# A three-branch attention and expert tower on one core: two casts change engine, and the work between batches is put in another order

## The chip, the cores and the metric

The kernel runs on one core of a Trainium2 chip. The metric is the device time of one execution in microseconds (us). A difference of about 0.3% is what a measurement of this kernel can tell from no change.

## What is computed

Eight sequences of 512 tokens are embedded (token, instruction and argument tables, then a layer norm) into 64 channels. Attention with 16 heads follows. Each head has one query (96 wide, 64 of them rotated by position) and three branches of keys and values: all earlier tokens, 128 tokens chosen by a score, and a window of 128 tokens. The three results are summed with one gate per batch and branch, projected, and added to the input. A layer norm and a mixture of eight experts (two per token) close the tower. Cut to the attention:

```python
        qr = _rope((cq @ Wq_rope).reshape(B, T, N_HEAD, ROPE).transpose(0, 2, 1, 3), cos, sin)
        q = jnp.concatenate([qn, qr], -1)
...
        o1 = _attn(q, k1, v1, causal[None, None])
...
        o2 = _attn(q, ks, vs)
...
        o3 = _attn(q, kw, vw, winmask[None, None])
```

## The kernel before, in words

**Precision.** Operands of the score, value and projection products are split into a high half in fp16 and a low half (the rest, in fp16), and three products stand for one.

**Loops.** Eight batches run one after the other, with 16 heads each. A head has four tiles of 128 queries. Each engine has its own program with the same loops (`heads`, then the last two heads, then `behind`, which holds the work between two batches). Every engine works through its own queue in order, and semaphores tie the queues together. One pass over a head is `turn` on TensorE (L1388), ScalarE (L647) and VectorE (L1090). At step t of four in the turn of head h, tile (t+3) mod 4 gets its scores, tile t+1 is transposed, and tile t gets its value product. So steps 1 to 3 already score tiles 0 to 2 of head h+1.

**A tile's way.** TensorE writes scores into one of two PSUM tiles S (L1336). VectorE masks them and takes the maxima (`maxima`, L996). ScalarE takes the exponentials (`probs`, L624). TensorE transposes them into PT (L1361, L1368). ScalarE takes the high half out (`take_hi`, L636) and VectorE the low half (`take_lo`, L1006). TensorE multiplies with the values (L1383). At a head's end VectorE normalises and gates the three branches (`combine`: a reciprocal L1013, the small product `coef` L1015 whose two inputs lie in SBUF, and L1018), and GpSimd adds the branches up (`branch_sum`, L472 and L474).

**Queries and keys of head h+2** are made during the turn of head h. TensorE projects the keys (`k_proj`, L1287) and the queries (`q_proj`, L1278) into the one tile X, and ScalarE copies each out (`evac_k`, `evac_q`, L565). GpSimd rotates them (L423, L424, L427, L428), casts them to fp16 (L456 the keys, L445 the queries) and subtracts that from the original for the low half (L459, L448). The sync engine then transposes `kparts` and `qparts` by DMA into `kh` and `qh` (L318, L327). TensorE needs both at step 1 of the next turn. GpSimd's order in one turn is: keys, queries, `low_values` (L479, the low half of the next head's values, whose high half is ScalarE's `high_values`), `branch_sum`. In the last batch `normalise` (L487 to L498) stands once in two turns between the queries and `low_values`. TensorE waits for its result when it transposes rows (L1348).

**Between two batches.** The last two heads of a batch also project the next batch's first two heads (`lead`). Nine value products (`value`, L1416) fill `vall`: 0 to 3 for all tokens, 4 to 7 for the window, 8 for the chosen ones. Four stand in the last head and five in `behind`. There TensorE also transposes the attention result (`attended`, L1442), scores the next head's tiles 0 and 1, projects the output (`project`, L1473), scores tile 2 and transposes tile 0. VectorE's `residual` (L1131) reads the projection, and TensorE waits for it at the end of `behind` (L1515).

Of the kernel before, what the change touches and what calls it, by code (L numbers as in the profile page):

```python
# [6 lines left out]
P = 128  # L7
# [25 lines left out]
def tower(nc, d, out):  # L33
# [5 lines left out]
    with ctx:  # L39
# [185 lines left out]
        VBANK = [S[0][:, 0:512], S[0][:, 512:1024], S[1][:, 0:512], S[1][:, 512:1024]]  # L225
        ZT = PT[:, 7 * P:8 * P]
# [140 lines left out]
        def _(g):  # L367
# [71 lines left out]
            def split_query(par, b, hh):  # L439
# [5 lines left out]
                g.tensor_copy(qparts[:, 0], qs[par][:]).then_inc(s["q_high"], 1)  # L445
                g.wait_ge(s["q_high"], H + 1)
# [3 lines left out]
            def split_key(par, b, hh):  # L450
# [5 lines left out]
                g.tensor_copy(kparts[:, 0, :, NOPE:P], kk[par][:, :, NOPE:P]).then_inc(s["k_high"], 1)  # L456
                g.wait_ge(s["k_high"], H + 1)
# [3 lines left out]
            def query(par, b, hh, x):  # L461
                rope_q(par, b, hh, x)
                split_query(par, b, hh)

            def key(par, b, hh, x):
                rope_k(par, b, hh, x)
                split_key(par, b, hh)
# [55 lines left out]

            def heads(b, rows=False):
                with g.Fori(0, NH // 2 - 1) as hp:
                    for par in range(2):
                        key(par, b, hp * 2 + (par + 2), xbase(b) + hp * 4 + x_index(par, "kp"))
                        query(par, b, hp * 2 + (par + 2), xbase(b) + hp * 4 + x_index(par, "qp"))
                        if rows and par == 0:
                            normalise(hp, xn_b[:])  # L530
                        low_values(1 - par, b, hp * 2 + (par + 1))
                        branch_sum(par, b, hp * 2 + par)
# [30 lines left out]
        def _(act):  # L563
# [48 lines left out]

            def high_values(par, b, hh):
# [33 lines left out]
            def turn(b, h, xb, p, last, nxt=None, rows=None):  # L647
# [3 lines left out]
                for t in range(NT):  # L651
                    u = p * NT + t
                    if t == 0 and last < 1:
                        evac_k(p, xb + x_index(0, "kp"), H + 1)
                        evac_q(p, xb + x_index(0, "qp"), H + 1)
                    if t == 2 and last < 2:
                        high_values(1 - p, b, h + 1)
                    if nxt is not None:
# [3 lines left out]
                    if nxt is not None and last == 2 and t >= 2:  # L662
                        if t == 2:
                            act.wait_ge(s["v_split"], b * NH + NH)
                        value(b + 1, (t - 2) * 2)
# [10 lines left out]
            def value(b, i):  # L676
                act.wait_ge(s["v_psum"], b * 9 + i + 1)
                if i < 4:
                    nc.scalar.activation(vall[:, i, :], VBANK[i % 4], ACT.Copy, scale=qkinv[:, 2:3]).then_inc(s["v_act"], 1)
                else:  # L680
                    copy(vall[:, i, :], VBANK[i % 4]).then_inc(s["v_act"], 1)
# [16 lines left out]
            def behind(b, nxt, U, first):  # L698
# [5 lines left out]
                value(b, 4)  # L704
# [16 lines left out]
            value(0, 0)  # L721
            value(0, 2)
# [60 lines left out]
        def _(dve):  # L783
# [239 lines left out]
            def value(b, i):  # L1023
                dve.wait_ge(s["v_psum"], b * 9 + i + 1)
                if i < 4:
                    v.tensor_scalar(vall[:, i, :], VBANK[i % 4], qkinv[:, 2:3], None, ALU.mult).then_inc(s["v_dve"], 1)
                else:
                    v.tensor_copy(vall[:, i, :], VBANK[i % 4]).then_inc(s["v_dve"], 1)
# [61 lines left out]
            def turn(b, H, p, last, nxt=None, rows=None):  # L1090

                U = H * NT
                for t in range(NT):
# [19 lines left out]
                    if nxt is not None and last == 2 and t >= 2:  # L1113
                        if t == 2:
                            dve.wait_ge(s["v_split"], H + 1)
                        value(b + 1, (t - 2) * 2 + 1)
# [16 lines left out]
            def behind(b, U, first):  # L1133
                value(b, 5)
# [6 lines left out]
                maxima(1, 1, U + 1)  # L1141
                if not first:
                    residual(b - 1)
                maxima(2, 2, U + 2)
                take_lo(0, 0, U)
# [5 lines left out]
            value(0, 1)  # L1151
            value(0, 3)
# [57 lines left out]
        def _(pe):  # L1210
# [177 lines left out]
            def turn(h, H, xb, p, last, b=None, nxt=None, rows=None):  # L1388
# [3 lines left out]
                for t in range(NT):  # L1392
                    u = p * NT + t
                    if last < 1 and t == 0:
                        k_proj(h + 2, xb + x_index(0, "kp"))
                    i = t if last == 1 else t + 4
# [7 lines left out]
                    if last < 1 and t == 0:  # L1404
                        q_proj(h + 2, xb + x_index(0, "qp"))
# [4 lines left out]
                    if nxt is not None and last == 2 and t >= 2:  # L1410

                        value(b, (t - 2) * 2)
                        value(b, (t - 2) * 2 + 1)
                    values(u, t, p, U + t, H)

            def value(b, i):  # L1416

                if i >= 4 and i % 2 == 0:
                    pe.wait_ge(s["v_act"], b * 5 + (i - 4) // 2 + 1)
                if i >= 4 and i % 2 == 1:  # L1420
                    pe.wait_ge(s["v_dve"], b * 4 + (i - 5) // 2 + 1)
                if i == 0:
                    pe.wait_ge(s["k1_moved"], b * 2 + 2)
                if i < 4:
                    for c, a in ((0, 0), (0, 1), (1, 0)):
                        last = mm(VBANK[i % 4], k1T[:, c, i * P:(i + 1) * P], wvh[:, a], start=(c + a == 0), stop=(c == 1))
                elif i < 8:
                    for a in range(2):
                        last = mm(VBANK[i % 4], xh[:, (i - 4) * P:(i - 3) * P], wvwh[:, a], start=(a == 0), stop=(a == 1))
                else:  # L1430
                    for a in range(2):
                        last = mm(VBANK[i % 4], selh[:], wvsh[:, a], start=(a == 0), stop=(a == 1))
                last.then_inc(s["v_psum"], 1)

            def behind(b, nxt, H, first):
# [9 lines left out]
                for i in range(4, 9):  # L1445
# [233 lines left out]
```

## Time and profile before

| what | value |
|---|---|
| time, median of 3 runs | 1868.04 us (1863.59 to 1869.03) |
| the profiled execution: its own time, its span | 1866.17 us, 1864.2 us |
| busy share: TensorE, VectorE, ScalarE, GpSimd | 76%, 79%, 65%, 77% |
| granted TensorE clock over the span, in the heads | 0.964, 1.00 |
| VectorE waits for TensorE's scores (L996) | 118.0 us in 142 waits |
| TensorE waits for the transposed queries (L1336) | 108.7 us in 98 waits |
| GpSimd waits for VectorE's combine (L472) | 53.6 us in 17 waits |
| transposed queries and keys, issue to landing | 3.0 us and 3.4 us |

The profile is of one execution. Its span runs from the first to the last instruction and is 2.0 us shorter than that execution's time, and its time is 1.9 us under the median. Four engines are busy about equally, so busy shares alone don't show what sets the pace. That has to be read from a turn's timeline and from who waits for whom.

### The profile page before, as it was taken

The page shows a single profiled execution, that of the slowest core. Times are in us where ns is not written, and L with a number is a line of the kernel's source. Part 1 is how long each engine was busy: PE and PEld are TensorE (multiplying, and loading weights), DVE is VectorE, ACT ScalarE, POOL GpSimd, SP SyncE. Part 2 cuts the span into 40 slices and gives each one's busy share as a digit, 9 for nine tenths or more (in the row PEclk, how much of TensorE's full clock was granted, in tenths as well). Part 3 has the DMA queues.
Part 4 walks back from the last instruction along what each step waited for, and adds up shares of the span by engine and source line. Part 5 has one row for each costly group of instructions (what it writes and reads, how often), then busy time and mean ns, then how long its engine had stood idle before and what let it go on. Part 6 is the DMA issues. An engine that isn't in the chain of part 4 may idle for free.

```text
span 1864.2 us, 64283 instructions
## 1 busy us (share of the span) xinstructions
PE 1417.9 (76%) x19368; PEld 1139.9 (61%) x19368; DVE 1474.7 (79%) x4982; ACT 1219.8 (65%) x3280; POOL 1436.9 (77%) x2126
## 2 busy tenths in 40 slices
PE   1041588888888888888888888888888888888878
PEld 0021476667776766676766677666767666767643
DVE  5738588878888788878887888788878887878745
ACT  0041377767776777767776777677767776777634
POOL 6775588868887788778877888688868887899610
PEclk9985799999999999999999999999999999999989
DMA  5110222222222222222222222222222221233200
GB/s 92 23 26 16 47 53 53 54 55 51 51 51 44 61 56 52 44 58 53 54 46 57 54 51 51 54 51 53 56 50 54 51 56 38 50 68 68 53 4 21
DMA packets 327553, 92.03 MB, mean 49 GB/s; under 512 B 321104, under 2 KB 323024, under 8 KB 327520
## 3 DMA queue, kind: packets, MB, share of 16 engines
q1 hardware_dynamic: 324448, 88.48, 24.1%
q0 software_dynamic: 3072, 3.15, 1.0%
q8 instruction: 15, 0.25, 0.1%
q14 instruction: 18, 0.15, 0.0%
HBM read 6.51 MB, written 1.05 MB: 4 GB/s over the span
## 4 chain that ended last, share of the span: by engine, by line
POOL 38%; DVE 21%; issue 18%; PE 10%; DMA 7%; POOLq 2%; ACT 1%; DVEq 1%; SPq 0%; ACTq 0%
DMA qh<-qparts 7%; DVE S L996 6%; POOL big L424 6%; POOL big L393 5%; DVE big L1006 5%; POOL big L423 4%; POOL kparts L459 4%; POOL qparts L448 3%; POOL kparts L456 2%; DVE negm L996 2%; POOL qparts L445 2%; POOL kk L427 2%; PE S L1336 2%; DVE coef L1015 2%; POOL kk L428 2%
## 5 line engine op out<-in xcount | busy, mean ns | idle before, releaser
L624 ACT ACTIVATE big<-S,negm 128x128 f32<-128x128 f32 (+3 forms) x1536 | 578.4, 454 | 116.9 <-DVE negm L996 116.9
L1006 DVE SCALAR_TENSOR_TENSOR big<-PT,big 128x384 f16<-128x384 f32 (+3 forms) x1024 | 477.5, 502 | 55.8 <-ACT big L636 41.1
L636 ACT ACTIVATE big<-PT 128x384 f16<-128x384 f32 (+3 forms) x1024 | 422.3, 453 | 141.1 <-PE PT L1361 107.0
L1336 PE MATMUL S<-k1T,qh 128*128 128x128 f16 (+3 forms) x1536 | 297.3, 302 | 122.6 <-DMA qh<-qparts 108.7
L996 DVE CUSTOM_DVE_ANT_0 S<-S,mask_c,unscale 128x128 f32<-128x128 f32 (+3 forms) x512 | 285.3, 557 | 129.5 <-PE S L1336 118.0
L1336 PE MATMUL S<-kh,qh 128*128 128x128 f16 (+1 forms) x3072 | 320.3, 241 | 0.0
L1383 PEld LDWEIGHTS O<-vh,big 128*128 128x128 f16 x8064 | 276.5, 96 | 22.8 <-DVE big L1018 8.6
L1383 PE MATMUL O<-vh,big 128*128 128x33 f16 x8064 | 282.8, 178 | 7.3 <-DVE big L1018 5.5
L1368 PE MATMUL PT<-cst,big 128*128 128x128 f32 x1408 | 246.9, 280 | 20.6 <-DVE big L1006 18.3
L1336 PEld LDWEIGHTS S<-kh,qh 128*128 128x128 f16 x3072 | 227.7, 99 | 56.5 <-issue 2.3
L1361 PE MATMUL PT<-cst,big 128*128 128x128 f32 x1280 | 230.3, 279 | 13.9 <-DVE big L1006 12.6
L996 DVE CUSTOM_DVE_ANT_0 S<-S,cst,kfix 128x256 f32<-128x256 f32 (+1 forms) x512 | 233.0, 455 | 0.0
L996 DVE DVE_READ_ACCUMULATOR2_ANT negm<- 128x1 f32 x1536 | 217.5, 142 | 0.2
L1336 PEld LDWEIGHTS S<-k1T,qh 128*128 128x128 f16 x1536 | 110.1, 98 | 162.3 <-issue 118.2
L1368 PEld LDWEIGHTS PT<-cst,big 128*128 128x128 f32 x1408 | 160.4, 142 | 51.2 <-issue 45.2
L996 DVE CUSTOM_DVE_ANT_0 S<-S,mask_c,kfix 128x128 f32<-128x128 f32 x512 | 181.6, 355 | 0.0
L1283 PE MATMUL X<-wqh,cqT 128*128 (+1 forms) x1536 | 116.6, 222 | 74.4 <-ACT kk L565 58.0
L565 ACT ACTIVATE qs<-X 128x512 f32<-128x512 f32 x128 | 76.6, 598 | 146.6 <-PE X L1283 146.6
L1361 PEld LDWEIGHTS PT<-cst,big 128*128 128x128 f32 x1280 | 146.8, 143 | 25.8 <-DVE big L1006 15.0
L448 POOL TENSOR_TENSOR qparts<-qs,qparts 128x512 f16<-128x512 f32 x128 | 148.1, 1157 | 18.6
L1283 PEld LDWEIGHTS X<-wqh,cqT 128*128 128x128 f16 x1536 | 91.8, 98 | 109.2 <-issue 105.7
L459 POOL TENSOR_TENSOR kparts<-kk,kparts 128x480 f16<-128x480 f32 x128 | 141.0, 1102 | 18.6
(295 smaller groups left out, 2449.2 us busy)
## 6 DMA issues: line engine op xcount, KB each, us to landing
lat_b<-lat_all SPq DMA_DIRECT2D x8, 448.0 KB, 3.1
qh<-qparts SPq DMA_TRANSPOSE x128, 3.0
kh<-kparts SPq DMA_TRANSPOSE x128, 3.4
xnT_all<-xnT_b SPq DMA_DIRECT2D x14, 128.0 KB, 2.5
xn_b<-xn_all SPq DMA_DIRECT2D x8, 128.0 KB, 2.8
xnT_b<-xnT_all SPq DMA_DIRECT2D x8, 128.0 KB, 2.3
out_dram<-h_all SPq DMA_DIRECT2D x8, 128.0 KB, 2.0
xn_all<-xn_b SPq DMA_DIRECT2D x7, 128.0 KB, 2.0
```

The lines of the kernel that those rows point to most:

```text
L424: g.tensor_tensor(tmp[:, 1, 0:tiles, :], v, sin5[:, 0:tiles, :], ALU.mult).then_inc(part, 1)
L448: g.tensor_tensor(qparts[:, 1], qs[par][:], qparts[:, 0], ALU.subtract).then_inc(s["q_split"], 1)
L459: g.tensor_tensor(kparts[:, 1, :, NOPE:P], kk[par][:, :, NOPE:P], kparts[:, 0, :, NOPE:P], ALU.subtract).then_inc(s["k_split"], 1)
L624: last = nc.scalar.activation(pr[par][:, lo:lo + n], S[par][:, lo:lo + n], ACT.Exp, bias=negm[par][:, k:k + 1], scale=-1.0)
L636: last = nc.scalar.activation(pT[par][:, 0, lo:lo + n], PT[:, lo:lo + n], ACT.Copy, scale=PSCALE)
L996: last = v.tensor_tensor_reduce(out=z, in0=z, in1=m, scale=unscale[:] if k == 0 else kfix[:], scalar=3.0e38, op0=ALU.add, op1=ALU.min, acc ...
L1006: v.scalar_tensor_tensor(pT[par][:, 1, lo:lo + n], PT[:, lo:lo + n], PSCALE, pT[par][:, 0, lo:lo + n], ALU.mult, ALU.subtract).then_inc(s[ ...
L1283: last = mm(X[:, t * QW:(t + 1) * QW], cqT[:, c, t * P:(t + 1) * P], wqh[:, a].rearrange("c h q -> c (h q)")[:, ds(h * QW, QW)], start=(c ...
L1336: last = mm(z[:, lo:lo + n], qh[par][:, c, t * P:(t + 1) * P], keys[:, a, :], start=(c + a == 0), stop=(c == 1))
L1361: last = tp(PT[:, lo:lo + P], src[:, lo:lo + P], ident)
L1368: last = tp(PT[:, lo:lo + P], src[:, lo:lo + P], ident)
L1383: last = mm(o, w[:, c, blocks[i] * P:(blocks[i] + 1) * P], vh[p][:, a, v0 + i, :], start=(j == 0), stop=(j == len(parts) - 1))
```

## The change

GpSimd no longer casts queries and keys in the turns of heads 0 to 13. ScalarE does it, at steps 2 and 3 of the turn. GpSimd's order in a turn is written anew (`prepare`), with the two additions of `branch_sum`, now of the head before, set between the steps of the rotation. `low_values` and, in the last batch, `normalise` stand at its end. On TensorE `q_proj` goes from step 0, behind the scores, to the start of step 1, and on ScalarE `evac_q` and `high_values` stand at the start of step 1. The value products come in another order (`VORDER`), six of them in the last head from step 1 on and three in `behind`. The output projection goes behind the scores of tile 2 and the transposes of tile 0, and `residual` with it. The work at the batch border on GpSimd stays as it was, casts included.

```diff
+        VORDER = [4, 5, 6, 7, 8, 0, 1, 2, 3]
...
+            def prepare(b, h, hh, par, rows=None, add=True):
+                x, H = xbase(b) + h * 2, b * NH + hh
...
+                g.wait_ge(s["x_evac"], x + x_index(0, "kp") + 2)
+                g.tensor_tensor(kt[:, 0], k[:, :, NOPE:HD], cos5, ALU.mult)
+                g.tensor_tensor(kt[:, 1], k[:, :, NOPE:HD], sin5, ALU.mult).then_inc(s["rope_tk"], 1)
+                if add:
+                    g.wait_ge(s["comb_done"], b * NH + h + 1)
...
+                    g.tensor_tensor(osum[:], o[:, :, 0, :], o[:, :, 1, :], ALU.add).then_inc(s["osum_part"], 1)
+                g.wait_ge(s["rope_tk"], H + 1)
...
+                g.wait_ge(s["x_evac"], x + x_index(0, "qp") + 2)
+                g.tensor_tensor(qt[:, 0, 0:NT], q[:, :, NOPE:HD], cos5[:, 0:NT], ALU.mult)
+                g.tensor_tensor(qt[:, 1, 0:NT], q[:, :, NOPE:HD], sin5[:, 0:NT], ALU.mult).then_inc(s["rope_tq"], 1)
+                if add:
...
+                    g.tensor_tensor(o_b[:, :, ds((h - 1) * VD, VD)], osum[:], o[:, :, 2, :], ALU.add).then_inc(s["osum_done"], 1)
+                g.wait_ge(s["rope_tq"], H + 1)
...
+                low_key(par, b, hh)
+                low_query(par, b, hh)
+                low_values(1 - par, b, hh - 1)
+                if rows is not None:
+                    normalise(rows, xn_b[:])
...
+            def high_key(par, H):
+                act.wait_ge(s["rope_k"], H + 1)
+                act.wait_ge(s["k_turned"], H * 16 + 16)
+                copy(kparts[:, 0, :, NOPE:P], kk[par][:, :, NOPE:P]).then_inc(s["k_high"], 1)
+            def high_query(par, H):
+                act.wait_ge(s["rope_q"], H + 1)
+                act.wait_ge(s["q_turned"], H * 16 + 16)
+                copy(qparts[:, 0], qs[par][:]).then_inc(s["q_high"], 1)
...
                     if t == 0 and last < 1:
                         evac_k(p, xb + x_index(0, "kp"), H + 1)
+                    if t == 1 and last < 1:
                         evac_q(p, xb + x_index(0, "qp"), H + 1)
-                    if t == 2 and last < 2:
+                    if t == 1 and last < 2:
                         high_values(1 - p, b, h + 1)
+                    if t == 2 and last < 1:
+                        high_key(p, H + 2)
+                    if t == 3 and last < 1:
+                        high_query(p, H + 2)
...
-                    if nxt is not None and last == 2 and t >= 2:
+                    if nxt is not None and last == 2 and t >= 1:
...
                     if last < 1 and t == 0:
                         k_proj(h + 2, xb + x_index(0, "kp"))
+                    if last < 1 and t == 1:
+                        q_proj(h + 2, xb + x_index(0, "qp"))
...
-                    if last < 1 and t == 0:
-                        q_proj(h + 2, xb + x_index(0, "qp"))
...
                 scores(1, 1, 0, H * NT + 1)
+                scores(2, 2, 0, H * NT + 2)
+                if not first:
+                    pe.wait_ge(s["oT_act"], b * 2)
+                    pe.wait_ge(s["oT_dve"], b * 2)
+                turn_probs(0, 0, H * NT)
                 if not first:
                     project(b - 1, H)
-                scores(2, 2, 0, H * NT + 2)
-                turn_probs(0, 0, H * NT)
```

## Rows read from the trace of the kernel before

**Rows 1.** Busy time by engine in one head's turn (window, us, busy us).

```profile
508.85:519.99 11.14, 9.11 (x145) 7.77 (x143) 9.97 (x38) 8.75 (x24) 9.92 (x16) 1.00 0.27 52
```

**Rows 2.** One of GpSimd's groups: busy us, mean ns | idle before, releaser.

```profile
L456 POOL CAST kparts<-kk 128x480 f16<-128x480 f32 x128 | 74.7, 584 | 33.7 <-POOL kk L428 33.4 <-DMA kh<-kparts 0.3
```

**Rows 3.** GpSimd's timeline: start us, length us, engine, line, operation.

```profile
513.68 0.73 POOL L423 TENSOR_TENSOR big<-qs,cst 128x256 f32<-128x256 f32 x1
...
516.25 0.61 POOL L445 CAST qparts<-qs 128x512 f16<-128x512 f32 x1 [0.19 <-POOL qs L428]
517.00 1.16 POOL L448 TENSOR_TENSOR qparts<-qs,qparts 128x512 f16<-128x512 f32 x1
518.12 0.71 POOL L479 TENSOR_TENSOR vh<-vall,vh 128x288 f16<-128x288 f16 x1
```

**Rows 4.** VectorE's timeline over two heads; idle before, releaser in brackets.

```profile
512.04 1.02 DVE L1006 SCALAR_TENSOR_TENSOR big<-PT,big 128x384 f16<-128x384 f32 x2
...
517.43 0.76 DVE L1015 TENSOR_TENSOR coef<-rinv,gate_all 128x12 f32<-128x12 f32 x1
...
518.79 0.75 DVE L996 CUSTOM_DVE_ANT_0 S<-S,mask_c,unscale 128x512 f32<-128x512 f32 x1
...
522.38 0.36 DVE L996 CUSTOM_DVE_ANT_0 S<-S,mask_c,unscale 128x128 f32<-128x128 f32 x1 [0.89 <-PE S L1336]
...
523.20 1.01 DVE L1006 SCALAR_TENSOR_TENSOR big<-PT,big 128x384 f16<-128x384 f32 x2
...
528.47 0.84 DVE L1015 TENSOR_TENSOR coef<-rinv,gate_all 128x12 f32<-128x12 f32 x1
...
530.20 0.76 DVE L996 CUSTOM_DVE_ANT_0 S<-S,mask_c,unscale 128x512 f32<-128x512 f32 x1 [0.20 <-issue]
```

**Rows 5.** ScalarE's timeline in the first of these heads.

```profile
511.51 0.87 ACT L636 ACTIVATE big<-PT 128x384 f16<-128x384 f32 x2 [0.49 <-PE PT L1361]
...
513.08 0.45 ACT L565 ACTIVATE vh<-vall 128x288 f16 x1
513.47 0.98 ACT L636 ACTIVATE big<-PT 128x512 f16<-128x512 f32 x2
...
515.41 0.29 ACT L636 ACTIVATE big<-PT 128x128 f16<-128x128 f32 x1
```

**Rows 6.** VectorE's timeline in the head before a batch ends.

```profile
575.68 0.75 DVE L996 CUSTOM_DVE_ANT_0 S<-S,mask_c,unscale 128x512 f32<-128x512 f32 x1
...
579.50 1.02 DVE L1006 SCALAR_TENSOR_TENSOR big<-PT,big 128x384 f16<-128x384 f32 x2 [0.47 <-ACT big L636]
```

**Rows 7.** ScalarE's timeline in the same head.

```profile
577.29 1.31 ACT L624 ACTIVATE big<-S,negm 128x512 f32<-128x512 f32 x3 [2.38 <-DVE negm L996]
578.48 0.61 ACT L565 ACTIVATE qs<-X 128x512 f32<-128x512 f32 x1
578.96 0.89 ACT L636 ACTIVATE big<-PT 128x384 f16<-128x384 f32 x2
```

**Rows 8.** The tile coef: ns min/median/max, first and last start.

```profile
L1015 DVE TENSOR_TENSOR coef<-rinv,gate_all x128: 170/754/867, 235.0 to 1783.8; 128x12 f32<-128x12 f32 x128
```

**Rows 9.** TensorE's timeline between two batches.

```profile
600.56 1.09 PE L1442 MATMUL PT<-cst,o_b 128*128 128x128 f32 x8 [0.65 <-POOL o_b L474]
...
604.80 3.79 PE L1473 MATMUL O<-wproj,oT 128*128 128x64 f32 x32 [0.89 <-ACT oT L565]
...
610.20 0.60 PE L1292 MATMUL X<-wkw,xh 128*128 x8 [0.30 <-issue]
```

**Rows 10.** VectorE's timeline, last batch: row statistics, two heads apart.

```profile
1640.42 0.59 DVE L1034 BATCH_NORM_STATS2 bst<-h_all 128x6 f32 x4
...
1665.00 0.60 DVE L1034 BATCH_NORM_STATS2 bst<-h_all 128x6 f32 x4
```

**Rows 11.** GpSimd's timeline, last batch: first and last step of a normalisation.

```profile
1645.44 0.23 POOL L493 TENSOR_SCALAR lnr<-lnmv 128x4 f32<-128x4 f32 x1
...
1647.45 0.61 POOL L498 TENSOR_TENSOR xn_b<-xn_b,lnr 128x256 f32<-128x256 f32 x1
```

More of the change, by code:

```diff
@@ L437, in rope_k, with high_query @@
                 rope(kk[par], rt[1], s["rope_tk"], s["rope_k"], 5, b * NH + hh + 1)
-            def split_query(par, b, hh):
+            def high_query(par, b, hh):
                 H = b * NH + hh
@@ L534, in _ @@
+            def heads(b, rows=False):
+                prepare(b, 0, 2, 0, 0 if rows else None, add=False)
+                with g.Fori(0, NH // 2 - 2) as hp:
+                    prepare(b, hp * 2 + 1, hp * 2 + 3, 1)
+                    prepare(b, hp * 2 + 2, hp * 2 + 4, 0, hp + 1 if rows else None)
+                prepare(b, NH - 3, NH - 1, 1)
+                branch_sum(1, b, NH - 3)
             with g.Fori(0, B - 1) as b:
@@ L720, in _ @@
                 lead(i, 0)
-            value(0, 0)
-            value(0, 2)
+            for j in range(0, 6, 2):
+                value(0, j)
             behind(0, 0, 0, True)
@@ L1112, in turn @@
                         choose(0, B - 1, t + 4, 1)
-                    if nxt is not None and last == 2 and t >= 2:
-                        if t == 2:
+                    if nxt is not None and last == 2 and t >= 1:
+                        if t == 1:
                             dve.wait_ge(s["v_split"], H + 1)
-                        value(b + 1, (t - 2) * 2 + 1)
+                        value(b + 1, (t - 1) * 2 + 1)
                 combine(p, b, H)
@@ L1141, in behind @@
                 maxima(1, 1, U + 1)
+                maxima(2, 2, U + 2)
+                take_lo(0, 0, U)
                 if not first:
                     residual(b - 1)
-                maxima(2, 2, U + 2)
-                take_lo(0, 0, U)
             split_rows(0)
@@ L1150, in _ @@
             split_keys(0, xbase(0) + x_lead("k1"))
-            value(0, 1)
-            value(0, 3)
+            for j in range(1, 6, 2):
+                value(0, j)
             behind(0, 0, True)
@@ L1409, in turn, with value @@
                         hidden(0, (2 * t - 2, 2 * t - 1))
-                    if nxt is not None and last == 2 and t >= 2:
-                        value(b, (t - 2) * 2)
-                        value(b, (t - 2) * 2 + 1)
+                    if nxt is not None and last == 2 and t >= 1:
+                        value(b, (t - 1) * 2)
+                        value(b, (t - 1) * 2 + 1)
                     values(u, t, p, U + t, H)
[L1416 to L1421, printed above, removed]
+            def value(b, j):
+                i = VORDER[j]
+                if j >= 4 and j % 2 == 0:
+                    pe.wait_ge(s["v_act"], b * 5 + (j - 4) // 2 + 1)
+                if j >= 4 and j % 2 == 1:
+                    pe.wait_ge(s["v_dve"], b * 4 + (j - 5) // 2 + 1)
                 if i == 0:
@@ L1443, in attended @@
                     last.then_inc(s["oT_psum"], 1)
-                for i in range(4, 9):
-                    value(b, i)
+                for j in range(6, 9):
+                    value(b, j)
                 if not first:
@@ L1505, in _ @@
             pe.wait_ge(s["ones_col"], 4)
-            for i in range(4):
-                value(0, i)
+            for j in range(6):
+                value(0, j)
             behind(0, 0, 0, True)
```

59 lines of the change are left out of this document (33 added, 26 removed).

## The prediction, made before the changed kernel ran

> **What bounds the kernel now.** I read the window of one head's turn first. A turn takes 11.14 us, and in it VectorE is busy for 9.97 us, GpSimd for 9.92, TensorE for 9.11 and ScalarE for 8.75 [rows 1]. No engine fills the turn by its busy time, so the next view is who waits. GpSimd waits in front of its casts, but for its own instruction before, the rotation it has just done: 33.4 of 33.7 us ahead of the key cast [rows 2], 0.19 us ahead of a query cast [rows 3]. Otherwise one step follows the other: a query cast of 0.61 us starts 0.75 us ahead of the subtraction, and that 1.12 us ahead of the next step [rows 3]. VectorE on the other hand stands still for 0.89 us in the turn until TensorE's scores come [rows 4], and these wait for the queries that GpSimd has finished last. So GpSimd's chain of 11.14 us is the pace of the 14 turns of each batch in which a head is prepared, 112 in all.
>
> **Part 1, the casts.** On GpSimd a turn loses 0.75 us for the query cast [rows 3] and 0.58 + 0.14 us for the key cast [rows 2, 3]. That leaves 11.14 - 0.75 - 0.72 = 9.67 us at most, less still where the additions fill the waits behind the rotation. GpSimd stops being the bound. On ScalarE a cast is not seen before. The nearest row is a copy of 512 elements out of PSUM, which holds the engine for 0.48 us and ends after 0.61 [rows 7]. A copy inside SBUF of 288 elements holds it for 0.39 us [rows 5], so SBUF is no cheap source. Below, a cast is not under that 0.39 us. Above, the farthest row is GpSimd's own subtraction at 1.16 us [rows 3]. I take 0.48 us, from the row of equal size, for each cast. ScalarE is then busy for 8.75 + 0.96 = 9.71 us, again under 11.14.
>
> **What is late next.** The chain that now decides runs from ScalarE to VectorE and back, since the copy of queries and `high_values` are moved to stand between the exponentials of tile 3 and `take_hi` of tile 2. From the start of VectorE's maxima of tile 3 to the exponentials 1.61 us pass (575.68 to 577.29) [rows 6, 7]. The exponentials take 1.19 us, the query copy 0.48 [rows 7], `high_values` 0.39 [rows 5]. From the start of `take_hi` to that of `take_lo` it is 0.54 us (578.96 to 579.50) [rows 6, 7]. From there VectorE runs on to `coef` in 5.39 us in one head and 5.27 in the next, mean 5.33. From the end of `coef` to the next maxima of tile 3 it is 0.60 and 0.89 us, mean 0.75 [rows 4]. Together 1.61 + 1.19 + 0.48 + 0.39 + 0.54 + 5.33 + 0.75 = 10.29 us, plus `coef` itself.
>
> `coef` is 12 elements wide, and takes 0.17 us at least but 0.75 in the median [rows 8]. In the first head it is seen to wait for GpSimd's subtraction: it starts at 517.43 and ends at 518.19, where the subtraction that began at 517.00 ends at 518.16 [rows 3, 4]. So its price depends on what GpSimd is at when VectorE gets there. Measured from the start of `take_lo` of tile 2, ScalarE's run of 3.90 us (511.51 to 515.41) begins 0.54 us earlier, loses `high_values` (0.39) and gains the key cast (0.48) [rows 5]. Then come the query cast (0.61), the hand-over (0.14) and GpSimd's subtraction (1.12) [rows 3, 7]: -0.54 + 3.90 - 0.39 + 0.48 + 0.61 + 0.14 + 1.12 = 5.32 us. There the subtraction ends and `low_values` starts, 0.71 us long. VectorE arrives at 5.27 in one head and 5.39 in the other. The first gets by with 0.17 us. The second waits until `low_values` ends, 5.32 + 0.71 - 5.39 = 0.64, plus 0.03, or 0.67 us. I take one of each, 0.42 us on average, as the two rows straddle the border. A turn is then 10.29 + 0.42 = **10.71 us**, a gain of 0.43. The ends are 10.46 (short in every head) and 10.96 (long in every head).
>
> The Trainium skill ("SBUF — State Buffer", section "Who interferes with whom") says that a VectorE instruction with two SBUF inputs and a GpSimd instruction that reads SBUF exclude each other, and whichever issues first holds the port to its end. The trace agrees with it in the 0.03 us between the two ends above. By that rule alone the order of issue in each head gives either 10.46 or 10.96 us and nothing between; the sum by the one is 1795 us and by the other 1844, which are two of the rivals below.
>
> **Other waits of the new order.** The queries still have a round of their own: cast 0.61, hand-over 0.14, subtraction 1.16 [rows 3, 7], then 4.22 us from its end to the next head's first maxima (518.16 to 522.38) and 0.82 to `take_lo` [rows 3, 4], then 3.45 us of ScalarE's run up to the cast (the sum above without its last three terms). That is 10.40 us, under 10.71, so the DMA transposes are covered with 0.31 us to spare, and the wait of 0.89 us shrinks rather than goes. `high_key` and `high_query` make ScalarE wait for GpSimd's rotation, with `take_hi` and `probs` queued behind and VectorE behind these. Counted from `take_lo` of tile 2, the query copy starts at -0.54 - 0.39 - 0.48 = -1.41 and ends at -0.80; the rotation takes 516.25 - 513.68 = 2.57 us [rows 3] and an addition of at most as much as one of its steps, some 0.7, stands in it, so GpSimd is through at 2.6 (hand-over included), and the cast comes at 3.45. This cover of 0.85 us lost, every us more is a us for ScalarE, and VectorE behind it. `branch_sum`, moved by most of a turn, frees its buffer for the combine two heads on, a turn early. `low_values` behind both subtractions ends at 6.03, ahead of the value product of the next turn, which follows the next maxima of tile 3 at 6.5. `q_proj` moved behind the transposes and value product of step 0 is hidden by ScalarE's exponentials, which its copy follows anyway. All these at nothing.
>
> **Part 2, between batches.** The value products are the same in number, six in the last head instead of four. TensorE waits for GpSimd's `o_b` for 0.65 us right behind them [rows 9], and that is late as before, so their gain is 0, at most 0.65. The projection holds TensorE for 3.79 us [rows 9]. Tile 2's scores and tile 0's transposes get ahead of it, but TensorE's wait for the residual now stands directly behind it, and the next turn's first projection (610.20) [rows 9] comes no earlier. What is gained is that VectorE's and ScalarE's work for these tiles is done by then. ScalarE's key copy no longer queues behind it, and VectorE loses one wait like the 0.89 us above [rows 4]. I take 0.6 us for each of 7 borders, 4 us, between 0 and 9.
>
> **Part 3, the last batch.** Two heads take 1665.00 - 1640.42 = 24.58 us there [rows 10], with a normalisation of 2.62 us on GpSimd (1645.44 to 1648.06) [rows 11]. It moves behind `low_values`, and TensorE's row transposes wait for it in the next turn. It ends 6.03 + 2.62 = 8.65 us after `take_lo`, or 2.2 us into a turn that starts at 6.5. Exponentials due 1.61 us into it then come at about 3.6, 2.0 us late. With the statistics on VectorE at about 1 us (0.59 us of them are in the row [rows 10], the rest I count at no more than that) a pair is 2 x 10.71 + 2.0 + 1.0 = 24.4 us, against 24.58. I take no gain for these 14 turns, between 6 us won (as in other batches, 14 x 0.43) and 5 lost.
>
> **The sum.** 98 turns x 0.43 = 42 us, plus 4 us, from the profiled execution's own 1866.2 us (span 1864.2, 2.0 around it): **1820 us**, 2.5% less. That execution stands 1.9 us under the median, which I leave out.
>
> **Rivals.**
> - `coef` short in every head, a turn of 10.46 us: 98 x 0.68 = 67, plus 4: 1795 us. For it speaks that any delay of ScalarE's cast by 0.1 us lets VectorE in first. Against it, the 5.39 of the other head. Chance 0.2.
> - `coef` long in every head, 10.96 us: 98 x 0.18 = 18, plus 4: 1844 us. It takes a cast shorter by 0.1 us. Chance 0.2.
> - No gain: `coef` at its longest, 0.87 us [rows 8], makes 11.16 us, and the change doesn't shorten a turn: 1862 us with the borders. Chance 0.09.
> - Slower: ScalarE becomes the bound. The key cast stands right ahead of the `take_hi` that VectorE's `take_lo` of tile 3 waits for, and the query cast right ahead of that for the next tile 0, so whatever they take beyond 0.48 us goes into the loop. At 1.0 us each, inside the bound of 1.16, a turn is 10.71 + 2 x 0.52 = 11.75 us, and 112 turns x 0.61 cost 68, less 4 at the borders: 1930 us. It decides from a cast of 0.48 + 0.43 / 2 = 0.70 us on. Against it speaks that the copy inside SBUF takes 0.45 us for 288 elements [rows 5], less than that out of PSUM for 512 [rows 7]. Chance 0.11.
>
> **How the numbers follow.** The forecast has 0.4, and the cases above 0.2, 0.2, 0.09 and 0.11. Faster by over 0.3% (about what a measurement of this kernel can tell from no change) is 0.4 + 0.2 + 0.2 = 0.80, the same 0.09, slower 0.11. The range runs from 1784 us (the short `coef`, with borders at 9 us and the last batch at 6 won: 1866 - 67 - 9 - 6) to 1853 us (the long one, with borders at 0 and the last batch 5 lost: 1866 - 18 + 5), and leaves out the last two cases.
>
> **What would show it.** Right: GpSimd at under 9.7 us busy in a turn of 10.5 to 11.0, with gaps ahead of its two subtractions that ScalarE ends; ScalarE waiting for VectorE's maxima ahead of tile 3's exponentials; VectorE waiting for ScalarE ahead of `take_lo` of tile 2; `coef` at two lengths; the projection directly ahead of a wait of TensorE for the residual. Wrong: casts on ScalarE over 0.70 us, ScalarE waiting for GpSimd's rotation at steps 2 or 3, or TensorE waiting for `qh` for longer than now.

## The result, and the profile after

The changed kernel takes 1853.81 us in the median of five runs (1852.4 to 1855.75), the kernel before 1869.03 (1863.59 to 1872.01) on the same chip. The ratio is 0.9924, 95% interval 0.9905 to 0.9942: 0.8% faster, where 2.5% was forecast. The profiled execution took 1852.40 us (span 1850.6), 13.8 us under that of before; 46 were forecast, and the time lies 0.8 us above the range. Some executions of the kernel before and of the experiments lie over 2% above the others at a lower granted clock (0.94 against 0.96), and medians and ratios leave them out.

The direction is right and the size is not, so the first question is which stretch the 13.8 us come from. VectorE's `residual` stands once in each batch. Its starts, from VectorE's timeline of either kernel, give the time of each batch:

```
             1st     2nd     3rd     4th     5th     6th     7th     8th     first to 7th / 7th to 8th
before     414.91  608.74  803.57  998.26 1193.21 1386.92 1581.73 1798.06   1166.82 / 216.33
changed    414.09  606.39  797.20  989.48 1180.33 1371.17 1562.04 1784.32   1147.95 / 222.28
```

Up to the first `residual` 0.8 us are won, in the six batches behind it 18.9, and in the last batch 6.0 are lost. Two heads of the changed kernel, in a window from one `coef` to the next but one (columns as in [rows 1], with the counts of instructions):

```profile
482.69:493.83 11.14, 9.83 (x148) 7.97 (x146) 9.70 (x35) 9.55 (x27) 8.70 (x15) 1.00 0.29 55
493.83:504.46 10.63, 9.14 (x141) 7.55 (x139) 9.50 (x36) 9.19 (x26) 8.49 (x14) 1.00 0.28 53
```

A turn takes (11.14 + 10.63) / 2 = 10.88 us, not 10.71. GpSimd (the last of the five busy times) fell from 9.92 to some 8.6 us and ScalarE rose from 8.75 to 9.4, as forecast. What the engines wait for is seen in three timelines. GpSimd:

```profile
490.40 1.08 POOL L466 TENSOR_TENSOR kparts<-kk,kparts 128x480 f16<-128x480 f32 x1
492.57 1.16 POOL L452 TENSOR_TENSOR qparts<-qs,qparts 128x512 f16<-128x512 f32 x1 [1.08 <-ACT qparts L603]
493.69 0.72 POOL L488 TENSOR_TENSOR vh<-vall,vh 128x288 f16<-128x288 f16 x1
...
503.30 1.16 POOL L452 TENSOR_TENSOR qparts<-qs,qparts 128x512 f16<-128x512 f32 x1 [1.08 <-ACT qparts L603]
504.42 0.72 POOL L488 TENSOR_TENSOR vh<-vall,vh 128x288 f16<-128x288 f16 x1
```

VectorE in the same heads (answering to [rows 4]):

```profile
484.28 0.76 DVE L1049 CUSTOM_DVE_ANT_0 S<-S,mask_c,unscale 128x512 f32<-128x512 f32 x1 [0.21 <-issue]
...
488.44 1.02 DVE L1059 SCALAR_TENSOR_TENSOR big<-PT,big 128x384 f16<-128x384 f32 x2 [0.56 <-ACT big L684]
...
493.83 0.60 DVE L1068 TENSOR_TENSOR coef<-rinv,gate_all 128x12 f32<-128x12 f32 x1
...
495.02 0.75 DVE L1049 CUSTOM_DVE_ANT_0 S<-S,mask_c,unscale 128x512 f32<-128x512 f32 x1
...
499.18 1.02 DVE L1059 SCALAR_TENSOR_TENSOR big<-PT,big 128x384 f16<-128x384 f32 x2 [0.26 <-ACT big L684]
...
504.46 0.70 DVE L1068 TENSOR_TENSOR coef<-rinv,gate_all 128x12 f32<-128x12 f32 x1
```

ScalarE in the first of them (answering to [rows 5, 7]):

```profile
485.90 1.31 ACT L672 ACTIVATE big<-S,negm 128x512 f32<-128x512 f32 x3 [0.88 <-DVE negm L1049]
487.10 0.60 ACT L603 ACTIVATE qs<-X 128x512 f32<-128x512 f32 x1
487.57 0.46 ACT L603 ACTIVATE vh<-vall 128x288 f16 x1
487.90 0.89 ACT L684 ACTIVATE big<-PT 128x384 f16<-128x384 f32 x2
...
489.39 0.67 ACT L603 ACTIVATE kparts<-kk 128x480 f16<-128x480 f32 x1
489.89 1.04 ACT L684 ACTIVATE big<-PT 128x512 f16<-128x512 f32 x2
490.73 1.18 ACT L672 ACTIVATE big<-S,negm 128x256 f32<-128x256 f32 x3
491.70 0.73 ACT L603 ACTIVATE qparts<-qs 128x512 f16<-128x512 f32 x1
492.22 0.65 ACT L684 ACTIVATE big<-PT 128x128 f16<-128x128 f32 x2
```

and its two groups of casts (busy us, mean ns | idle before):

```profile
L603 ACT ACTIVATE qparts<-qs 128x512 f16<-128x512 f32 x112 | 80.9, 723 | 0.0
...
L603 ACT ACTIVATE kparts<-kk 128x480 f16<-128x480 f32 x112 | 74.0, 661 | 0.0
```

The loop is there as forecast: VectorE waits for ScalarE ahead of `take_lo` of tile 2, ScalarE for VectorE ahead of tile 3's exponentials. GpSimd, though, stands still for 1.08 us ahead of `low_query`, because the cast comes late, and `low_values` (L488) starts right behind that. VectorE reaches `coef` 0.14 us after that start in one head and 0.04 in the other. `coef` then takes 0.60 and 0.70 us, and ends 0.02 us after `low_values` (494.43 against 494.41, and 505.16 against 505.14). So it is long in both heads, not in one. The same shows over the whole run (answering to [rows 8]):

```profile
L1068 DVE TENSOR_TENSOR coef<-rinv,gate_all x128: 170/597/708, 235.9 to 1769.8; 128x12 f32<-128x12 f32 x128
```

Between two batches TensorE (answering to [rows 9]):

```profile
597.48 1.09 PE L1496 MATMUL PT<-cst,o_b 128*128 128x128 f32 x8 [1.53 <-POOL o_b L483]
...
602.55 3.68 PE L1530 MATMUL O<-wproj,oT 128*128 128x64 f32 x32
607.85 0.60 PE L1345 MATMUL X<-wkw,xh 128*128 x8 [1.61 <-issue]
```

The values done sooner only lengthen the wait for `o_b` (0.65 to 1.53 us), and behind the projection TensorE now waits 1.61 us for the residual and the loop's end, against 0.30. From the first of these rows to the last it is 10.37 us, against 9.64. In the last batch TensorE waits for the normalised rows, and VectorE's statistics are 25.18 us apart (1596.37 to 1621.55), against 24.58 [rows 10]. Here are `take_lo` of tile 2, tile 1's exponentials, the query cast, GpSimd's wait for it, VectorE's next maxima of tile 3, the last step of the normalisation, TensorE's wait for it, and the exponentials of tile 3:

```profile
1595.43 1.02 DVE L1059 SCALAR_TENSOR_TENSOR big<-PT,big 128x384 f16<-128x384 f32 x2 [0.77 <-ACT big L684]
...
1598.71 1.10 ACT L672 ACTIVATE big<-S,negm 128x256 f32<-128x256 f32 x3 [0.80 <-DVE negm L1049]
1599.69 0.64 ACT L603 ACTIVATE qparts<-qs 128x512 f16<-128x512 f32 x1
...
1600.47 1.16 POOL L452 TENSOR_TENSOR qparts<-qs,qparts 128x512 f16<-128x512 f32 x1 [2.00 <-ACT qparts L603]
...
1602.41 0.76 DVE L1049 CUSTOM_DVE_ANT_0 S<-S,mask_c,unscale 128x512 f32<-128x512 f32 x1
...
1604.26 0.61 POOL L507 TENSOR_TENSOR xn_b<-xn_b,lnr 128x256 f32<-128x256 f32 x1
...
1605.02 0.38 PE L1393 MATMUL PT<-cst,xn_b 128*64 128x128 f32 x2 [2.76 <-POOL xn_b L507]
...
1606.63 1.29 ACT L672 ACTIVATE big<-S,negm 128x512 f32<-128x512 f32 x3
```

### The profile page after: what moved, and what is told of

Read it like the earlier page. It is cut to its first block, busy times and chain, and to the rows that moved or that the text cites. A ratio compares the mean times of both kernels' runs of the same rounds, so it can differ in the third digit from the quotient of the medians.

```text
span 1850.6 us, 63902 instructions
## 1 busy us (share of the span) xinstructions
PE 1436.8 (78%) x19368; PEld 1137.6 (61%) x19368; DVE 1461.7 (79%) x4982; ACT 1299.4 (70%) x3504; POOL 1289.5 (70%) x1902
## 4 chain that ended last, share of the span: by engine, by line
DVE 23%; issue 19%; PE 17%; ACT 16%; POOL 13%; DMA 8%; ACTq 2%; DVEq 1%; POOLq 0%; SPq 0%
DVE S L1049 9%; DMA qh<-qparts 7%; ACT big L672 7%; POOL big L394 5%; PE S L1389 5%; ACT big L684 4%; DVE big L1059 4%; DVE negm L1049 3%; POOL qparts L452 3%; DVE coef L1068 2%; ACT vh L603 2%; PE PT L1421 2%; PE O L1530 2%; ACT qparts L603 2%; PE PT L1414 1%
## 5 line engine op out<-in xcount | busy, mean ns | idle before, releaser
L672 ACT ACTIVATE big<-S,negm 128x128 f32<-128x128 f32 (+3 forms) x1536 | 586.8, 473 | 200.8 <-DVE negm L1049 200.6
L1059 DVE SCALAR_TENSOR_TENSOR big<-PT,big 128x384 f16<-128x384 f32 (+3 forms) x1024 | 472.2, 501 | 80.0 <-ACT big L684 57.2
L684 ACT ACTIVATE big<-PT 128x384 f16<-128x384 f32 (+3 forms) x1024 | 431.1, 490 | 69.3 <-PE PT L1414 65.8
L1436 PEld LDWEIGHTS O<-vh,big 128*128 128x128 f16 x8064 | 272.7, 96 | 44.9 <-DVE big L1071 30.3
L540 POOL TENSOR_TENSOR big<-kk,cst 128x320 f32<-128x320 f32 x112 | 96.5, 862 | 95.5 <-ACT kk L603 95.5
L550 POOL TENSOR_TENSOR big<-qs,cst 128x256 f32<-128x256 f32 x112 | 81.3, 726 | 81.4 <-ACT qs L603 81.4
```

Source lines behind the costliest of these rows:

```text
L540: g.tensor_tensor(kt[:, 0], k[:, :, NOPE:HD], cos5, ALU.mult)
L672: last = nc.scalar.activation(pr[par][:, lo:lo + n], S[par][:, lo:lo + n], ACT.Exp, bias=negm[par][:, k:k + 1], scale=-1.0)
L684: last = nc.scalar.activation(pT[par][:, 0, lo:lo + n], PT[:, lo:lo + n], ACT.Copy, scale=PSCALE)
L1059: v.scalar_tensor_tensor(pT[par][:, 1, lo:lo + n], PT[:, lo:lo + n], PSCALE, pT[par][:, 0, lo:lo + n], ALU.mult, ALU.subtract).then_inc(s[ ...
L1436: last = mm(o, w[:, c, blocks[i] * P:(blocks[i] + 1) * P], vh[p][:, a, v0 + i, :], start=(j == 0), stop=(j == len(parts) - 1))
```

## The experiments

All ratios are to the kernel before on the same chip; the changed kernel's is 0.9924.

**1. `low_values` ahead of `low_query`.**

```diff
                 low_key(par, b, hh)
-                low_query(par, b, hh)
                 low_values(1 - par, b, hh - 1)
+                low_query(par, b, hh)
```

> In GpSimd's turn low_values is put ahead of low_query, into the gap of 1.08 us in which GpSimd waits for the query cast; nothing else changes. Theory (coef waits for the low_values that GpSimd has just started when VectorE arrives, in every head): coef then meets the end of low_query, falls from 0.60-0.70 us to about 0.17-0.2 in both heads, the turn from 10.88 to about 10.45 us (there the queries' own round binds), and the time by 112 x 0.43 = 48 us, to about 1806 us. Rival 1 (the turn is held by the queries' round or by ScalarE already, and coef only fills a wait): coef gets short and the time stays at 1854 us within 5. Rival 2 (coef is long because of what else reads SBUF, not because of low_values): coef stays at 0.6-0.7 us and the time at 1854.

1820.23 us, ratio 0.9750 (0.9732 to 0.9768). `coef` is short in every head:

```profile
L1068 DVE TENSOR_TENSOR coef<-rinv,gate_all x128: 170/172/173, 238.5 to 1741.0; 128x12 f32<-128x12 f32 x128
```

The theory's cause holds, both rivals fall, and the size was too large: a turn takes 10.57 us (10.22 and 10.93 in turn), since TensorE now waits longer for the queries ahead of the first scores (0.69 and 0.71 us in the changed kernel):

```profile
671.24 0.34 PE L1389 MATMUL S<-k1T,qh 128*128 128x128 f16 x3 [0.76 <-DMA qh<-qparts]
...
682.05 0.34 PE L1389 MATMUL S<-k1T,qh 128*128 128x128 f16 x3 [1.14 <-DMA qh<-qparts]
```

That is the queries' round of the forecast, put at 10.40 us. The borders took some of the gain as well: in the profiled execution the granted clock of TensorE fell behind each of the seven (0.72 in the 6 us from the start of the `residual` on), and a border took 26.4 us from its last `coef` to the next batch's first, against 25.0 where the clock stayed at 1.00. In the changed kernel this happens at two of seven borders, in the kernel before also at two. The profiled execution is the slowest of the five, though (1826.96 us), so the others may have lost the clock less often.

**2. Projection and residual in their old place.**

```diff
                 scores(1, 1, 0, H * NT + 1)
-                scores(2, 2, 0, H * NT + 2)
...
-                turn_probs(0, 0, H * NT)
                 if not first:
                     project(b - 1, H)
+                scores(2, 2, 0, H * NT + 2)
+                turn_probs(0, 0, H * NT)
```

(VectorE's `residual` goes ahead of tile 2's maxima accordingly.)

> Projection and residual go back to their old place, ahead of tile 2's scores and maxima; all else as in the changed kernel. Theory (the move gains nothing: what VectorE and ScalarE win on tiles 2 and 0 is given back by TensorE's wait for the residual, directly behind the projection): within 5 us of the changed kernel, 1849 to 1859 us; the wait of TensorE of 1.61 us ahead of the next key projection goes, a wait of VectorE for tile 2's scores comes. Rival (the prediction's 0.6 us a border): 7 x 0.6 = 4 us slower, about 1858, and each border shows it. Rival 2 (the move costs): 7 x 1 us faster, about 1847.

1851.14 us, ratio 0.9915 (0.9896 to 0.9934). The time can't tell this from the changed kernel, but the batches can: where the border kept its clock, `residual` to `residual` takes 190.1 us, against 190.85 in the changed kernel, with the same turns in both. TensorE's wait ahead of the key projection is 0.30 us again. So the move costs some 0.75 us a border, as in rival 2; the forecast's gain of 0.6 is refuted.

**3. Normalisation ahead of `low_values`** in the last batch, as before the change.

```diff
-                low_values(1 - par, b, hh - 1)
                 if rows is not None:
                     normalise(rows, xn_b[:])
+                low_values(1 - par, b, hh - 1)
```

> In the last batch the normalisation goes back ahead of low_values; all else as in the changed kernel. Theory (the place behind low_values makes TensorE wait 2.76 us for the normalised rows, 0.9 us a pair more than hidden): pairs of 25.9 us fall to about 25.0, 7 x 0.9 = 6 us less, about 1848 us. Rival (the casts on ScalarE make the last batch slow, wherever the normalisation is): 1854 us within 2, since low_values is then late by 2.6 us and the value product waits for it.

1847.75 us, ratio 0.9898 (0.9877 to 0.9919). The time is the theory's, but the intervals overlap with those of the changed kernel. The last batch in the trace is 217.87 us from `residual` to `residual`, against 222.28. That is the theory's size less a little: 4.4 us of 6. TensorE's wait for the rows only falls from 2.76 to 2.10 us, so the place is not all of it.

**4. Projection behind tile 2's scores, ahead of tile 0's transposes.**

```diff
                 scores(2, 2, 0, H * NT + 2)
                 if not first:
-                    pe.wait_ge(s["oT_act"], b * 2)
-                    pe.wait_ge(s["oT_dve"], b * 2)
-                turn_probs(0, 0, H * NT)
-                if not first:
                     project(b - 1, H)
+                turn_probs(0, 0, H * NT)
```

(`residual` goes ahead of tile 0's `take_lo`.)

> The projection goes behind tile 2's scores but ahead of tile 0's transposes, the residual ahead of tile 0's take_lo; all else as in the changed kernel. Theory (TensorE's 1.6 us ahead of the next key projection is the wait for the residual, which stands last): that wait shrinks to under 0.5 us, each border gives 0.5 to 1 us, 4 to 7 us in all, about 1848 us. Rival (the border is held by ScalarE's and VectorE's work on tiles 0 to 3, and TensorE's wait is spare): 1854 us within 3.

1855.26 us, ratio 0.9944 (0.9922 to 0.9966): nothing is won in the time, as the rival says. The theory's wait shrinks only from 1.61 to 1.32 us, though, and it is not all spare: batches with an undisturbed border take 190.6 us, against 190.85 (experiment 2, with a wait of 0.30 us, has 190.1). Three borders instead of two lost the clock.

**5. Casts back on GpSimd**, all else as changed.

```diff
+                high_key(par, b, hh)
+                high_query(par, b, hh)
                 low_key(par, b, hh)
                 low_query(par, b, hh)
...
-                    if t == 2 and last < 1:
-                        high_key(p, H + 2)
-                    if t == 3 and last < 1:
-                        high_query(p, H + 2)
```

> Both casts go back to GpSimd, behind the rotations and ahead of the two subtractions; ScalarE's new order of copies, the interleaved rotations, and all else stay as in the changed kernel. Theory A (the gain comes from the order, and GpSimd has room for the casts once nothing waits for ScalarE's): the gap of 1.08 us goes, low_query ends about 0.6 us sooner behind the key rotation, coef gets past low_values at least in one head, a turn takes 10.4 to 10.7 us, and the time is 1810 to 1840 us. Rival (the prediction's part 1: GpSimd with the casts is the bound again, 8.5 us of steps, 1.3 of casts and its waits for the copies): turns of 11.0 to 11.2 us, 1863 to 1880 us.

1846.96 us, ratio 0.9886 (0.9870 to 0.9902), faster than the changed kernel. The rival, which was part 1 of the forecast, falls: with the new order GpSimd has room for both casts. Theory A is right in kind and too bold: the gap ahead of `low_query` is gone, but VectorE still meets `low_values` (`coef` 528 ns in the median), and turns take 10.84 us (10.72 and 10.96), but for five of 12.2 us in which the granted clock fell (0.86):

```profile
485.22 1.17 POOL L452 TENSOR_TENSOR qparts<-qs,qparts 128x512 f16<-128x512 f32 x1
486.33 0.73 POOL L488 TENSOR_TENSOR vh<-vall,vh 128x288 f16<-128x288 f16 x1
487.74 0.86 POOL L540 TENSOR_TENSOR big<-kk,cst 128x320 f32<-128x320 f32 x1 [0.69 <-ACT kk L605]
```

The last batch is shorter by 11.5 us (210.79), where nothing waits for a late cast. From the first `residual` to the seventh it is 1147.79 us, as in the changed kernel (1147.95). So the gain of the change does not need ScalarE's casts: the order that came with them gives as much without. GpSimd's waits for its own previous step, 78.9 us in the kernel before, are 7.2 us here.

**6. No interleaving on GpSimd** (`rope_k`, `rope_q`, the two subtractions, `low_values`, then the whole `branch_sum`; casts on ScalarE).

```diff
-                g.wait_ge(s["x_evac"], x + x_index(0, "kp") + 2)
-                g.tensor_tensor(kt[:, 0], k[:, :, NOPE:HD], cos5, ALU.mult)
...
+                rope_k(par, b, hh, x + x_index(0, "kp"))
+                rope_q(par, b, hh, x + x_index(0, "qp"))
                 low_key(par, b, hh)
                 low_query(par, b, hh)
                 low_values(1 - par, b, hh - 1)
+                if add:
+                    branch_sum(1 - par, b, h - 1)
```

> In prepare the two rotations and the branch sum are no longer interleaved: key rotation, query rotation, low_key, low_query, low_values, and the whole branch sum last; casts stay on ScalarE. Theory (interleaving only fills short waits of GpSimd, which is not the bound; and the query rotation ends sooner without the sums): the turn stays at 10.88 us within 0.1, the time at 1854 us within 8. Rival (the sums, now last, push GpSimd's next key rotation behind ScalarE's copy, and ScalarE's cast waits for the rotation): ScalarE waits for GpSimd ahead of a cast, turns of over 11 us, over 1866 us.

1861.67 us, ratio 0.9979 (0.9961 to 0.9996). In seven batches the theory holds: turns of 10.62 and 11.13 us, batches of 191.0. The time is at the very end of its bounds all the same: the loss sits in the last batch (228.93 against 222.28 us), which neither side had named.

**7. The first experiment, the projection's old place, and `branch_sum` sooner between batches.**

```diff
-                query(1, b + 1, 1, xbase(b + 1) + x_lead("qp1"))
+                rope_q(1, b + 1, 1, xbase(b + 1) + x_lead("qp1"))
+                high_query(1, b + 1, 1)
                 branch_sum(1, b, NH - 1)
+                low_query(1, b + 1, 1)
```

> low_values ahead of low_query as in the first experiment, projection and residual in their old place, and between batches branch_sum of the last head ahead of low_query of the next batch's second head (TensorE waits 1.53 us for o_b there). Theory (the border is held by o_b, and the projection's move costs 0.77 us a border): o_b comes 1.15 us sooner, each border is shorter by 1.15 + 0.77 = 1.9 us, 13 us in all under the first experiment, about 1807 us. Rival (the border is held by something else, such as the queries and keys of the next batch's heads): 1820 us within 4.

1801.65 us, ratio 0.9645 (0.9629 to 0.9661). TensorE's wait for `o_b` falls from 1.53 to 0.47 us, and an undisturbed border (last `coef` to the next batch's first) from 25.0 to 23.2 us, where 1.9 were expected. The projection's place gave 0.75 of these in experiment 2, so the rest is `o_b`: that it holds the border is shown. That the time came out under 1807 fits the clock: in the profiled executions one border of seven lost it here, and all seven in the first experiment.

**8. The query cast one step sooner on ScalarE**, on top of the first experiment.

```diff
-                    if t == 3 and last < 1:
-                        high_query(p, H + 2)
...
                         take_hi(u + 1, (t + 1) % NT, U + t + 1, rows)
+                    if t == 2 and last < 1:
+                        high_query(p, H + 2)
```

> low_values ahead of low_query as in the first experiment, and ScalarE's query cast one step sooner, ahead of tile 1's exponentials instead of behind them. Theory (with coef short, the turn of 10.57 us is held by the queries' round, cast to subtraction to DMA to scores and back): the round gets shorter by some 0.5 to 1 us, TensorE's waits of 0.76 and 1.14 us for qh shrink, the loop of VectorE and ScalarE binds at 10.4 to 10.5 us, 112 x 0.1 = 11 us less, about 1809 us. Rival (the loop through the exponentials is as tight, and tile 1's exponentials are late by the cast's 0.5 us): turns of 10.6 to 10.9 us, 1823 to 1855 us.

1807.49 us, ratio 0.9681 (0.9662 to 0.9699). The time is as the theory said, for another reason. A turn falls only to 10.54 us (10.20 and 10.88): the waits for `qh` shrink (0.45 and 0.85 us), and the loop of VectorE and ScalarE takes over at once (over the run VectorE waits 119.2 us for scores, not 162.1, but 60.8 us for ScalarE ahead of `take_lo`, not 34.3). The gain is in the last batch, where the normalisation on GpSimd waits for the cast: from its first `coef` to its last it takes 174.5 us, not 187.0. From `residual` to `residual` it is 203.33 against 219.25, but 3 of these 15.9 us lie behind the last `coef`, where the first experiment's profiled execution had a granted clock of 0.63 and this one 0.76.

**9. The query cast one step sooner, alone**, with `low_values` behind `low_query` as in the changed kernel (the diff of the eighth on the changed kernel).

> The changed kernel with one move alone: ScalarE's query cast goes ahead of tile 1's exponentials; low_values stays behind low_query. Theory (coef is long only because GpSimd starts low_values just ahead of it): low_query then starts 0.9 to 1.0 us sooner, low_values ends at about the time at which coef starts, coef falls to about 0.17 us without low_values having been moved, turns are at 10.54 us, and the time is within 6 us of the run with both moves, 1802 to 1814 us; the last batch gets its rows sooner and gives some 15 us of this. Rival (it takes low_values ahead of low_query): coef stays at 0.5 to 0.7 us, turns stay over 10.8 us, the time is 1838 to 1850 us.

1806.42 us, ratio 0.9673 (0.9658 to 0.9688): the theory in all its numbers. GpSimd:

```profile
477.00 1.16 POOL L452 TENSOR_TENSOR qparts<-qs,qparts 128x512 f16<-128x512 f32 x1
478.12 0.71 POOL L488 TENSOR_TENSOR vh<-vall,vh 128x288 f16<-128x288 f16 x1
480.34 0.86 POOL L540 TENSOR_TENSOR big<-kk,cst 128x320 f32<-128x320 f32 x1 [1.51 <-ACT kk L603]
```

and VectorE:

```profile
478.88 0.22 DVE L1066 RECIPROCAL rinv<-O 128x12 f32<-128x12 f32 x1
479.13 0.17 DVE L1068 TENSOR_TENSOR coef<-rinv,gate_all 128x12 f32<-128x12 f32 x1
```

`low_values` ends at 478.83, ahead of `coef`, and `coef` takes 171 ns in the median. Neither instruction was changed or moved against its neighbours on its own engine; only the moment differs. Turns take 10.55 us, the last batch 205.73.

**10. All moves that helped** (the seventh and the eighth together).

> All moves that helped: low_values ahead of low_query, projection and residual in their old place, the branch sum ahead of low_query between batches, and the query cast ahead of tile 1's exponentials. Theory (they act in different stretches and add up): 1801.7 us of the combination less the 11.8 us that the sooner cast gave, about 1790 us; turns 10.54, borders like those of the combination, the last batch some 15 us shorter. Rival (the sooner cast's gain was in borders and is had already): 1798 to 1803 us.

1784.87 us, ratio 0.9558 (0.9546 to 0.9571), 4.4% under the kernel before and the best of all. They add up, and a little more: no border lost its clock (every batch is 184.0 to 184.2 us), and the last batch takes 202.97.

## Why the prediction was right in kind and wrong in size

- **What was right.** GpSimd was the pace and no longer is. ScalarE never waits for a rotation: its casts show no idle time ahead of them. The loop summed to 10.29 us without `coef`; measured it is 10.88 - 0.65 = 10.23, and it holds term by term: the one that differs by more than 0.02 us is `high_values` (0.33 us, 487.57 to 487.90, not 0.39). The queries' round comes next (10.40 forecast, 10.57 seen where it binds). TensorE's wait for `o_b` takes all that the earlier values won. Of the signs that were named, two did not come: `coef` at two lengths, and a gap ahead of both subtractions (only `low_query` waits).
- **The step that failed first: "I take one of each", `coef` at 0.42 us.** It measured 0.60 and 0.70, mean 0.65, and 98 turns x 0.23 = 23 us of the forecast are gone, less the 6 us that the shorter loop gives back (98 x 0.06). The sum had the subtraction end 5.32 us after the start of `take_lo` of tile 2, and VectorE come at 5.27 and 5.39. Measured, VectorE comes at 5.28 and 5.39, as said, but the subtraction ends at 5.25 and 5.24 (493.69 - 488.44, 504.42 - 499.18). The cast ended later than its row (0.73 us, not 0.61) but began 3.26 us after `take_lo`, not 3.45: ScalarE's run from `take_hi` to the cast took 3.80 us (487.90 to 491.70), not the 3.99 of the sum. An error of 0.07 us put the head that should have been first behind `low_values`. The rival "`coef` long in every head" had this mechanism, and its 10.96 us a turn is near the 10.88 measured. Experiments 1 and 9 show the cause, each by another move. The Trainium skill ("SBUF — State Buffer", section "Who interferes with whom") calls the port that VectorE and GpSimd share an exclusive lock; the ends 0.02 us apart agree with it, but the 23 products named in the last section, which did not wait, do not.
- **The cast's price.** Assumed 0.48 us of ScalarE's time, it holds the engine for 0.50 (keys, 489.39 to 489.89) and 0.52 us (queries, 491.70 to 492.22), and it ends after 0.67 and 0.73. The time for which it holds the engine is what the loop pays, and that is under the 0.70 from which the rival "slower" decides.
- **The border, "I take 0.6 us".** The sign was wrong. The text saw TensorE's wait for the residual directly behind the projection, and priced it at nothing because the key projection "comes no earlier". It comes later by 10.37 - 9.64 = 0.73 us, and experiment 2 gets 0.75 back. Over seven borders that is 5 us lost, not 4 won.
- **The last batch, "I take no gain".** Six us were lost, one more than the bound of 5. Between the first and the last `coef` of the batch it is 7.6 us (186.85 to 194.40); the kernel before lost 1.9 us more on the way from the `residual` to that first `coef` (15.21 against 13.35), where its granted clock had fallen. The forecast added the statistics (1.0 us) to the pair, but not to the road to the query cast: ScalarE's tile 1 exponentials wait 0.80 us behind them, the cast comes 4.26 us after `take_lo` (1599.69 - 1595.43), and the normalisation ends at 9.44, not 8.65. The exponentials of the next tile 3 come 4.22 us behind their maxima (1602.41 to 1606.63), where 3.6 were forecast. Experiment 8, which lets the cast go first, is worth some 12.5 us there.
- **The sum, again.** 98 x 0.26 = 25.5, less 7 x 0.75 = 5.3, less 6.0 for the last batch makes 14.2 us; the two profiled executions differ by 13.8. Of the 32 us that are missing from the 46, the turns hold 17, the borders 9 (4 won forecast, 5 lost) and the last batch 6.

## What to carry to other kernels

A price that has two values, depending on which of two engines arrives first, isn't to be averaged: if the arrivals are nearer to each other than the sum is exact (0.07 us here), the forecast has to allow for the bad value in every turn, and the change to make is the one that pulls the arrivals apart. A cast moved to a less busy engine is not free for the engine it left: GpSimd waited about 1.08 us for it in a turn, and issuing it one step sooner was worth 47 us, 17 of them in the last batch. When work is put behind a long instruction, look at what then stands last ahead of the loop's next start.

## What the runs showed of the hardware

A product of 12 elements a partition on VectorE took 0.17 us or up to 0.71 in the changed kernel, by what GpSimd was at: 104 of 128 started within `low_values` and ended 0.02 or 0.03 us after it. Not every GpSimd instruction holds it up. In the last batch of experiment 8 the product took 0.17 us inside the 1.04 us of the normalisation's 128x4 power (L505), as it did in all 23 such meetings in four of the traces. Why it did not wait there is open:

```profile
1590.80 1.04 POOL L505 TENSOR_TENSOR lnr<-lnr,cst 128x4 f32<-128x4 f32 x1
...
1591.22 0.17 DVE L1068 TENSOR_TENSOR coef<-rinv,gate_all 128x12 f32<-128x12 f32 x1
```

ScalarE's cast of 128x512 inside SBUF took 0.73 us to its end, its copy of the same size out of PSUM 0.61. Behind some borders TensorE's granted clock fell to 0.50, the lower of its two levels (1.2 GHz):

```profile
795.00:798.00 3.00, 2.05 (x19) 1.91 (x18) 0.61 (x2) 1.03 (x3) 0.00 (x0) 0.96 1.03 284
798.00:801.00 3.00, 2.33 (x16) 1.48 (x17) 0.00 (x0) 0.57 (x1) 0.62 (x1) 0.50 0.29 66
801.00:804.00 3.00, 3.00 (x29) 2.80 (x28) 1.92 (x8) 1.17 (x3) 2.06 (x4) 0.50 0.00 0
```

This window of the changed kernel lies right behind the third `residual` (797.20), and TensorE was busy for 2.05 of the 3 us at whose end the clock fell; the batch took 1.4 us longer than an undisturbed one. In the profiled executions it happened at 2 of 7 borders before and after the change, at all 7 in the first experiment, and at none in the last, where TensorE's idle stretches at the border are shorter (0.47, 0.89 and 0.30 us, against 1.53 and 1.61). The seventh experiment has nearly the same short stretches and lost one border, and in the last batch the clock fell several times in every kernel (mean 0.92 to 0.97). What decides it was not tried and stays open; so does which part of the new order brings the gain that experiment 5 keeps.
